# Recommendation kernel on Trainium2: layer 0 of the first chunk tile by tile in float32 beside the attention, the image tower split in two

## The reference

```
img    = gelu(layernorm(item_emb @ mm_w + mm_b))          # image tower
target = item_table[item_id] + img
seq    = item_table[item_seq]                              # 50 rows per item
scores = relu([t, seq, t - seq, t * seq] @ aw1 + ab1) @ aw2 + ab2, masked where item_seq == 0
hist   = softmax(scores) @ seq
sparse = [like, view, id, img, hist], each scaled by a small gate (SE)
bil    = 10 products (se_i @ bil_W[i]) * se_j
x0     = [sparse, bil]                                     # 15 features x 128 = 1920 wide
x1     = x0 * (x0 @ K[0] + b0) + x0 ;  x2 = x0 * (x1 @ K[1] + b1) + x1
out    = sigmoid(w3 . gelu(ln(gelu(ln(x2 @ w1 + b1)) @ w2 + b2)) + b3)
```

## Time and profile before

| | us |
|---|---|
| median of 3 runs | 2104.42 (2103.35 to 2104.58) |
| the profiled execution | 2105.34, its span 2103.0 |
| PE busy | 1936.4 (92%) |
| DVE busy | 1337.0 (64%) |
| ACT busy | 903.0 (43%) |
| POOL busy | 893.9 (43%) |
| mean granted TensorE clock | 0.939 |

### The profile page before, as it was taken

The page is one execution under the profiler, slowest core; times in us unless marked ns, Lnnn a source line. Parts: engine busy times, 40 slices in busy tenths (PEclk is TensorE's granted clock), DMA queues, the critical chain, the costliest instruction groups (busy, mean ns, idle before and its releaser), DMA issues. The chain is left out here.

```text
span 2103.0 us, 32483 instructions
## 1 busy us (share of the span) xinstructions
PE 1936.4 (92%) x9608; PEld 1522.7 (72%) x9608; DVE 1337.0 (64%) x2248; ACT 903.0 (43%) x1927; POOL 893.9 (43%) x854
## 2 busy tenths in 40 slices
PE   1766658999999999999999999999999999999997
PEld 1444436778777887777777887777777888888886
DVE  4555555677778756667778755667778654445553
ACT  1443442545445244664544335654445243322234
POOL 7777777667566401657557302647550000000000
PEclk7666568999999999999999999999999999999998
DMA  5112113334344452334434452334432343333320
GB/s 164 50 49 53 48 52 98 104 111 137 115 121 121 137 174 79 96 90 142 117 111 132 129 182 71 100 96 140 116 106 88 116 167 126 93 96 97 98 68 1
DMA packets 99675, 220.27 MB, mean 105 GB/s; under 512 B 21792, under 2 KB 27184, under 8 KB 99376
## 3 DMA queue, kind: packets, MB, share of 16 engines
q1 hardware_dynamic: 63072, 136.90, 21.5%
q0 software_dynamic: 27136, 55.63, 10.4%
q10 hardware_dynamic: 9296, 25.70, 3.3%
HBM read 205.29 MB, written 12.85 MB: 104 GB/s over the span
## 5 line engine op out<-in xcount | busy, mean ns | idle before, releaser
L445 POOL DMA_INDIRECT e<-in_item_table,idx_all x800 | 843.7, 1055 | 649.4 <-POOLq L467 416.1
L870 ACT ACTIVATE Wh<-raw 128x640 fp32r<-128x640 f32 (+1 forms) x411 | 293.8, 723 | 508.9 <-ACTq L869 506.5
L1225 DVE TENSOR_TENSOR Wl<-raw,Wh 128x640 fp32r<-128x640 f32 (+1 forms) x411 | 331.9, 808 | 278.1 <-DVEq L1224 276.1
L586 PE MATMUL psum<-X0h,Wh 128*128 128x512 f32 x900 | 361.3, 401 | 1.3 <-PEq L584 1.3
L586 PE MATMUL psum<-X1h,Wh 128*128 128x512 f32 x900 | 357.1, 397 | 0.0
L587 PE MATMUL psum<-X0l,Wh 128*128 128x512 f32 x900 | 351.4, 390 | 0.0
L588 PE MATMUL psum<-X0h,Wl 128*128 128x512 f32 x900 | 351.1, 390 | 0.0
L587 PE MATMUL psum<-X1l,Wh 128*128 128x512 f32 x900 | 350.9, 390 | 0.0
L588 PE MATMUL psum<-X1h,Wl 128*128 128x512 f32 x900 | 350.4, 389 | 0.0
L829 ACT ACTIVATE e<-e,pw 128x128 f32<-128x128 f32 x800 | 242.8, 388 | 15.3 <-ACTq L142 15.3
L586 PEld LDWEIGHTS psum<-X0h,Wh 128*128 128x128 f32 x900 | 169.4, 188 | 36.5 <-issue 3.4
(11 more groups left out here) (159 smaller groups left out, 2168.2 us busy)
## 6 DMA issues: line engine op xcount, KB each, us to landing
raw<-in_cross_K SPq DMA_DIRECT2D x360, 320.0 KB
raw<-in_w SPq DMA_DIRECT2D x51, 256.0 KB
e<-in_item_table,idx_all POOLq DMA_INDIRECT x800, 2.5
dnn_scratch<-dn ACTq DMA_DIRECT2D x12, 960.0 KB
x1f<-dnn_scratch ACTq DMA_DIRECT2D x3, 2048.0 KB, 9.8
x1f<-dnn_scratch ACTq DMA_DIRECT2D x3, 1792.0 KB, 15.6
e<-in_w SPq DMA_DIRECT2D x9, 256.0 KB, 4.8
dn<-in_embT SPq DMA_DIRECT2D x1, 1024.0 KB, 5.4
```

The lines of the kernel that those rows point to most:

```text
L445: nc.gpsimd.indirect_dma_start(out=dst, out_offset=None, in_=table, in_offset=bass.IndirectOffsetOnAxis(ap=idx_all[:, t, s:s + 1], axis=0) ...
L586: m0 = mm(out, wh, Xh[:, 0:T, k, :], start=(k == 0), stop=False)
L870: af(Wh[:, split_slot(w), 0:n], raw[:, rs, 0:n], ACT.Copy).then_inc(hi_done, 1)
L1225: v.tensor_tensor(Wl[:, rs, 0:n], raw[:, rs, 0:n], Wh[:, slot, 0:n].bitcast(F32), ALU.subtract).then_inc(lo_done, 1)
```

## The change

Layer 0 of chunk 0 is no longer computed for four tiles at once from split operands. It is computed for one tile at a time, in float32 (`solo_products`: 128 columns, one matmul where there were three, over four times as many steps). The plan is now: an opening for tile 0 alone (13 steps); 45 **early** steps, which are the 15 features of layer 0 for tiles 0, 1 and 2; then chunk 0, whose first 15 steps are the same for tile 3, and whose steps 15 to 29 are layer 1 as before. I number the 60 solo steps s0 to s59; s45 is step 0 of chunk 0, and layer 1 begins at s60.

- The groups of tiles 1 to 4 stand at s-2 (an opening step), 0, 1, 3, 5; 8, 11, 14, 17, 20; 23 to 35 and 38 to 50 in threes (`SPREAD`). Tiles 5, 6 and 7 have theirs at steps 8 to 12, 14 to 18 and 20 to 24 of chunk 0 (before: 7 to 11, 13 to 17, 19 to 23, with tile 4 at 1 to 5). Chunks 1 to 3 have the groups where they were.
- The weights of the eight even features stay in SBUF (`kept`, the space of X0h and X1h), loaded once in 24 blocks; those of the seven odd ones are loaded anew for each tile through the ring `raw`. TensorE waits for a raw block itself; nothing is split, so Wh and Wl start with layer 1 (steps s59 on).
- After a feature VectorE scales 128 columns (`solo_scale`). x0 stays whole in x0f. In s52 to s59 the finished x1 is split for layer 1, two features a step.
- The tail of tiles 0 to 3 writes straight into x0f instead of dn, and `tail_hi` and `tail_lo` are gone.
- The image tower: one matmul batch and bias for all tiles, then statistics, norm and gelu for tile 0 alone; the other 15 tiles' statistics, norm, affine and gelu are in opening steps 3, 4, 5 and 6. Tile 0's image feature goes to S without the way through memory.
- The gathers of tile 1's features come after tile 0's last rows.

The diff, cut to its core:

```diff
-LAST = TILES[0] - 1
+OPEN = 1
+LAST = OPEN - 1
...
+PASSES = TILES[0] - 1
+KEPT = 8
+LOOSE = (FEATS - KEPT) * UNITS
+SHIFT = PASSES * LOOSE - KEPT * UNITS
+WHOLE = SHIFT + FEATS * UNITS
+FULL = 2 * (TPC - 1)
+HALVES = {FULL + 2 + q: (2 * q, 2 * q + 1) for q in range(FEATS // 2)}
+SPREAD = ((-2, 0, 1, 3, 5), (8, 11, 14, 17, 20), (23, 26, 29, 32, 35), (38, 41, 44, 47, 50))
 
 
 GROUP_STEPS = {
     4: [[1 + 6 * j + g for g in range(NG)] for j in range(4)],
+    0: [[s + g for g in range(NG)] for s in (8, 14, 20)],
...
+    def __init__(self, chunk, k, early=None):
         self.chunk, self.k = chunk, k
         self.layer, self.n = (None, None) if chunk is None else divmod(k, FEATS)
+        self.solo = early if early is not None else PASSES if chunk == 0 and self.layer == 0 else None
+        self.prev = self.last = None
+        if self.solo is not None:
+            self.last = (self.solo, self.n - 1) if self.n else (self.solo - 1, FEATS - 1) if self.solo else None
+        elif chunk is not None and (chunk, k) == (0, FEATS):
+            self.last = (PASSES, FEATS - 1)
+        elif chunk is not None:
+            self.prev = (chunk, self.layer, self.n - 1) if self.n else (chunk, 0, FEATS - 1) if self.layer else None
+        self.early = early is not None
...
-    for j in range(TILES[0]):
+    for j in range(OPEN):
         where.append([lead + NG * j + g for g in range(len(groups(j)))])
+    where += [[open_steps + k for k in ks] for ks in SPREAD]
     for c in range(1, CHUNKS):
-        at = open_steps + STEPS * (c - 1)
-        where += [[at + k for k in ks] for ks in GROUP_STEPS[TILES[c]]]
+        at = early_steps + STEPS * (c - 1)
+        where += [[at + k for k in ks] for ks in GROUP_STEPS[TILES[c] if c > 1 else 0]]
...
-        if t < TILES[0]:
+        if t < OPEN:
             fetch, aim, swing = max(s - 5, 0), s - 3, s - 2
         else:
 
-            fetch, aim, swing = s - 6, s - 4, s - 1
+            fetch, aim, swing = (s - 3, s - 2, s - 1) if t == OPEN else (s - 6, s - 4, s - 1)
         plan[fetch].fetch = plan[aim].aim = plan[swing].swing = plan[s - 1].share = plan[s].neg = t
 
-        gate = last + 2 if t < TILES[0] else last + 3
+        gate = last + 2 if t < OPEN else last + 3
         plan[last + 2].fold = plan[gate].gate = plan[gate + 1].lift = plan[gate + 2].pair = t
...
-        X0h = sb("X0h", [P, TPC, FEATS, P], F32R)
-        X1h = sb("X1h", [P, TPC, FEATS, P], F32R)
+        kept_at = -(-nc.sbuf_base // 32) * 32
+        kept = sb("kept", [P, KEPT, FEATS, P])
+        assert nc.sbuf_base == kept_at + 8 * TPC * FEATS * P and KEPT == 2 * TPC
+        X1h = nc.alloc_sbuf_tensor_at("X1h", [P, TPC, FEATS, P], F32R, offset=kept_at)
+        X0h = nc.alloc_sbuf_tensor_at("X0h", [P, TPC, FEATS, P], F32R, offset=kept_at + 4 * TPC * FEATS * P)
...
+            for b in range(KEPT * UNITS):
+                if b > 1:
+                    sp.wait_ge(kept_landed[b % 2], b // 2 * DMA)
+                n, kg = divmod(b, UNITS)
+                sp.dma_start(kept[:, n, kg * KG:(kg + 1) * KG, :].rearrange("p f b -> p (f b)"), kx_d[2 * n * UNITS + kg]).then_inc(kept_landed[b % 2], DMA)
...
+            def solo_products(a, n, kg):
+                out = xps[:, bank(a, n), 0:P]
+                if kg == 0:
+                    pe.wait_ge(bank_free, 1).then_inc(bank_free, -1)
+                loose = n % 2
+                if not loose:
+                    def block(i):
+                        return kept[:, n // 2, kg * KG + i, :]
+                else:
+                    w = a * LOOSE + n // 2 * UNITS + kg
+                    rs = raw_slot(w)
+                    pe.wait_ge(raw_landed[rs], DMA).then_inc(raw_landed[rs], -DMA)
+
+                    def block(i):
+                        return raw[:, rs, i * P:(i + 1) * P]
+                for i in range(KG):
+                    k = kg * KG + i
+                    if n == 0:
+                        pe.wait_ge(x_ready, 1).then_inc(x_ready, -1)
+                    last = mm(out, block(i), x0f[:, a, k, :], start=(k == 0), stop=(k == FEATS - 1))
+                    if i == 0 and loose and w:
+                        last.then_inc(w_free, 1)
+                if kg == UNITS - 1:
+                    last.then_inc(mm_done, 1)
+
+            def products(p, kg):
+                if p.solo is not None:
+                    solo_products(p.solo, p.n, kg)
+                    return
+                c, layer, n = p.chunk, p.layer, p.n
 
...
+            if opening[-1].open:
+                pe.wait_ge(hscore_free, 1).then_inc(hscore_free, -1)
+                score()
+            for i in range(2):
+                pe.wait_ge(kept_landed[i], KEPT * UNITS // 2 * DMA)
+            for p in early:
+                step(p)
...
-            def images():
+            def images_sd(a, b):
                 act.wait_ge(img_var, 1).then_inc(img_var, -1)
-                af(img_sd, img_mv[:, :, 1], ACT.Sqrt, bias=eps[:]).then_inc(img_sd_ready, 1)
+                af(img_sd[:, a:b], img_mv[:, a:b, 1], ACT.Sqrt, bias=eps[:]).then_inc(img_sd_ready, 1)
+
+            def images_first():
+                images_sd(0, 1)
                 act.wait_ge(img_norm, 1).then_inc(img_norm, -1)
-                flat = dn[:].rearrange("p t n -> p (t n)")
-                af(flat, flat, ACT.Gelu).then_inc(img_gelu, 1)
-                act.wait_ge(img_gelu, 1).then_inc(img_gelu, -1)
-                act.dma_start(img_d.rearrange("t p n -> p t n"), dn[:]).then_inc(img_stored, DMA)
-                act.wait_ge(img_stored, DMA)
+                done(af(S[:, 0, 3, :], dn[:, 0, :], ACT.Gelu))
+                act.sem_inc(img_landed[0], DMA)
+
+            def images_gelu():
+                act.wait_ge(img_norm, 1).then_inc(img_norm, -1)
+                rest = dn[:, 1:ntiles, :].rearrange("p t n -> p (t n)")
+                done(af(rest, rest, ACT.Gelu))
+                act.dma_start(img_d[1:ntiles].rearrange("t p n -> p t n"), dn[:, 1:ntiles, :]).then_inc(img_stored, DMA)
 
             def head_fetch(t):
                 b = t % SBUFS
+                if t == OPEN:
+                    act.wait_ge(img_stored, DMA)
                 act.dma_start(S[:, b, 3, :], img_d[t]).then_inc(img_landed[b], DMA)
 
 
...
-                if p.pair is not None:
-                    tail_hi(p.pair)
+                if p.k == 4:
+                    images_sd(1, ntiles)
+                if p.k == 6:
+                    images_gelu()
...
-                if p.n or p.layer:
-                    x_hi(*((c, p.layer, p.n - 1) if p.n else (c, 0, FEATS - 1)))
+                for n in p.split:
+                    x_hi(c, p.prev[1] if p.prev else 0, n)
...
+            def images_first():
+                dve.wait_ge(img_mm, 1).then_inc(img_mm, -1)
+                psum = flat[:, 0:ntiles * EMB].rearrange("p (t n) -> p t n", n=EMB)
+                done(v.tensor_tensor(dn[:], psum, img_rows[:, 0:1, :].to_broadcast([P, ntiles, EMB]), ALU.add))
...
+            def solo_scale(a, n):
+                dve.wait_ge(mm_done, 1).then_inc(mm_done, -1)
+                v.scalar_tensor_tensor(out=x1f[:, a, n, :], in0=xps[:, bank(a, n), 0:P], scalar=col("cb", n), in1=x0f[:, a, n, :],
+                                       op0=ALU.add, op1=ALU.mult).then_inc(scaled, 1)
+
+            def solo_end(a, n):
+                dve.wait_ge(scaled, 1).then_inc(scaled, -1)
+                dve.sem_inc(bank_free, 1)
+                if a == PASSES and n >= FULL:
+                    dve.sem_inc(xnew_ready, FULL + 1 if n == FULL else 1)
+
             def x_sum(c, layer, n):
                 T = TILES[c]
+                if c == 0:
+                    return
                 v.tensor_tensor(fresh(c, layer, n), X0h[:, 0:T, n, :].bitcast(F32), X0l[:, 0:T, n, :].bitcast(F32),
                                 ALU.add).then_inc(sum_done, 1)
 
             def x_scale(c, layer, n):
-                dve.wait_ge(sum_done, 1).then_inc(sum_done, -1)
+                if c:
+                    dve.wait_ge(sum_done, 1).then_inc(sum_done, -1)
...
+                if p.k == 3:
+                    images_stats(1, ntiles)
+                if p.k == 4:
+                    images_norm(1, ntiles)
+                if p.k == 5:
+                    images_affine(1, ntiles)
...
+                if p.last:
+                    solo_scale(*p.last)
+                elif p.prev:
+                    x_scale(*p.prev)
...
+                for n in p.split:
+                    x_lo(c, p.prev[1] if p.prev else 0, n)
+                if not p.early:
+                    unit_out(c, 3 * k + 1)
```

More of the change, by code:

```diff
@@ L103, in make_plan @@
     lead = 3
-    open_steps = lead + sum(len(groups(t)) for t in range(TILES[0])) + 4
+    open_steps = lead + sum(len(groups(t)) for t in range(OPEN)) + 4
+    early_steps = open_steps + PASSES * FEATS
     plan = [Step(None, k) for k in range(open_steps)]
+    plan += [Step(0, k, a) for a in range(PASSES) for k in range(FEATS)]
```

(38 more changed lines are left out.)

166 lines of the change are left out of this document (77 added, 89 removed).

## The result

| | before | changed |
|---|---|---|
| median, us | 2104.5 (2103.35 to 2106.47, 4 runs) | 2128.69 (2125.91 to 2128.84, 4 runs) |
| ratio | | 1.0111 (95% interval 1.0093 to 1.0128) |
| span of the profiled execution | 2103.0 | 2126.7 |
| mean granted clock | 0.939 | 0.958 |

A forecast was written before the change was run, and what follows sets the result against it. Before, gathers and latency bound the opening, matmuls the rest; changed, the chain through VectorE decides. +6.5 to s60's end, +4.4 and +1 make +12 us on 2105.34: 2117, median 2116 us; range 2088 to 2150.

The forecast's parts named there:

- Term A: Opening, now tile 0 alone, paid in gathers and tail: s0 starts at 126 us (122 to 131), against 327.4.
- The solo matmul: Float32 matmul of 128 columns in the solo steps: two passes, 0.223 us each, 3.35 us a solo step.
- Term B: From s0 to VectorE having written teT of tile 2's first group: reached at 202 us.
- Term C: Fifteen group cycles of 16.6 us plus 3 x 8.8: 275 us, to teT of tile 5's first group at 477.
- the plain ring: Chain of waits from one group's teT through the engines to the next in solo steps: forecast 16.6 us.
- the tile extras: VectorE's head_aim, tail_fold, head_neg, pair products and tail copy in the same chain: 8.8 us a tile (4 to 10).
- rival 2: Clock falls in solo steps: up to 2200 us, or 2135 if only tile borders and seam fall; chance 0.12 above forecast.
- Term D: Seam, s53 to s60's end, with five groups in a row and splits for layer 1: 83.7 us, ending at 561.
- Terms E and F: After s60: one more group behind step 15, +4.4 us, and tile 7's pair in the last step, +1 (0 to 5).
- 1, the chain doesn't bind: In s8 to s57 gathers and TensorE bind instead, cycle 14.45 us: about 2030 to 2045; chance 0.13 in full.
- 3, another rate or late raw blocks: Solo matmuls stream at another rate, adding 0.25 us a cycle (2120), or raw blocks come late; no separate case.
- 4, nearly nothing: s0 at 122, cycle 16.2 us, Term E hidden: 2104 us; chance 0.13 with neighbours within 0.2%.

The follow-up runs named there:

- run 6: Changed kernel with the image tower's statistics, norm and gelu for all 16 tiles put back ahead of the attention: 2130.21 us.
- run 2: Changed kernel with the history reduce executed twice for each group of tiles 2 to 4: 2178.05 us.
- run 4: Changed kernel with head_aim of tiles 3 to 5 one step earlier: 2114.76 us.
- run 8: run 1 with tail_fold of tiles 1 to 3 one step later, behind hidden_max, and gate, lift and pairs following: 2093.1 us, ratio 0.9956.
- run 9: run 8 with the target's transpose of tiles 2 to 5 and head_aim of tiles 3 to 5 one step earlier: 2077.03 us, ratio 0.9877.
- run 1: Changed kernel with history of tiles 1 to 4 one step later, behind the next group's teT; fold, gate, lift and pairs follow: 2106.48 us.
- run 3: Changed kernel with five float32 matmuls repeated in 13 solo steps that hold neither transposes nor hidden: 2127.43 us.
- run 7: Changed kernel with the edits of run 1 and run 4, tile 5's history late too and tail_pairs behind times_target in solo steps: 2130.17 us.

## Why the prediction was right in sign and wrong in size

The steps in the order of the prediction, forecast and measured:

- **Term A**, s0 at 126: 124.2. That the opening is bounded by gathers and tail was right, and so was that the kept blocks are no term. The last kept block is issued at 53.1 and lands within 7.3 us. The tower's other tiles cost nothing, as run 6 confirms from the other side.
- **The solo matmul** at 0.223 us: between starts, ten matmuls (20 rows) take 2.33 us in the ring, 0.233 each. By the rate of the Trainium skill that I set against it (page "TensorE: Matmul & The Clock Gate", section "Back-to-back issue gap": about 81 ns per matmul at 128 columns), taken for each pass, the ten would by estimate take 1.62 us; the trace decides for the row.
- **Term B**, te of tile 2's first group at 202: 202.5.
- **Term C is the step that failed, by its size**: 275 us forecast for three tiles, 289.0 measured (202.5 to 491.5; 97.0, 95.1 and 96.9 a tile). Of the 14 us, 5 are the plain ring, 16.93 for 16.6: the products 0.10, from acc to the end of teT 0.13, softmax to acc 0.10, fifteen times. The other 8.5 are the tile extras: 12.3, 10.5 and 12.3 over five plain rings, instead of 8.8. The operations themselves were sized well, if anything too high: aim 3.1, fold 2.4, neg 0.7, pairs 1.7, 7.9 together. What I put at nothing here (Term B had 2 us a cycle for it) was the clock behind the waits that they cause. Behind aim hidden begins 0.7 us late and takes 4.11 us instead of 2.31 (2.5 us a tile), and behind the wait for head_share products and transposes run at half rate, for which teT still waited 0.91 (297.96). Tile 2 has 1.3 us more in the ring before, where hidden began 0.9 late and took 2.77 us behind a wait of 2.00; tile 4 has 1.3 more in its last ring, a split of X1l (1.31 us) that stands ahead of the teT at 489.98. I had priced the falling clock, as the milder form of rival 2 (2135), but as an alternative to the chain, and it is a consequence of it; the mean clock of 0.95 between 200 and 480 shows it. Runs 2, 4 and 8 show the price: each us that VectorE adds on the ring costs 1.3 to 1.9 us (49.4 for 38.1; 13.9 for 9.3; 13.4 for three folds of 2.4).
- **Term D**, the seam, 83.7: 82.4 (491.5 to 573.86). Its shape was right: the five te lie 7.0, 13.2, 14.3 and 11.9 us apart, forecast 7.0, 13.4, 15.1 and 11.9, and the rest took 36.0, forecast 34.8. But the granted clock was 0.89 there and my sum had full clock, so part of this agreement is luck: some of my terms were too high.
- **Terms E and F**, together 5.4: s60's end to chunk 1 took 230.45, before 225.30, so 5.15; from chunk 1 to the end -0.4.
- Sum: +6.5 forecast to the end of s60, +19.0 measured; 19.0 + 5.15 - 0.4 = 23.7, the difference of the spans (2126.7 - 2103.0).

The rivals: 1, the chain doesn't bind, is refuted by run 2 (each reduce added in full) for this order, and run 9 shows that neither the gathers nor TensorE set its pace, since the same gathers and products fit into 81 us a tile; but the point that I gave for it, "below 15.5 it is a gain", nearly held: run 1 has a plain ring of 15.3 and came out level, because its borders were long. 3, another rate or late raw blocks: the rate cost 0.1 us a ring; run 3 excludes that TensorE's work binds in these steps, and the raw blocks, which it left alone, are in time for the faster pace of run 9. 4, nearly nothing, lies outside the interval. GpSimd's idle time appeared as forecast; the changed kernel's waits between 200 and 480 (line, cause, us in total, times, longest):

```profile
POOL e L487 <- POOLq L507: 61.9, 10, 9.1
...
PE psum L632 <- PEq L616: 18.4, 6, 4.7
```

What stays open: the 8 us of tile 5's late history in run 7, and the seam, where s53 to layer 1 takes 60 to 68 us in every version.

## What to carry to other kernels

When a change shortens the work that covers a latency (here about 10.4 us of products a step became 3.5), write down the ring of each in-order queue before and after: what stands in it that nobody waits for (here a reduce of 2.39 us, a fold, a transposed target behind ten weighings) can be moved behind the instruction that is waited for, and the order, not the amount of work, then makes 52 us (2128.69 to 2077.03). Move one thing at a time: two edits that gained 22 and 14 us alone gained 19 together, and a plausible third lost 13. Price a wait of TensorE with the clock behind it, not by its length.
